# Moving a share of dense work into a fifth stage of a graph network, with a third-layer term computed early

## The reference

```python
h = jnp.maximum(_layernorm(x, axis=-1), 0.0)
x = x + _L0_gnn_ref(h, src, dst, W_neigh1, W_self1, b_self1, ...)   # three layers of:
    neigh_sum = segment_sum(h[src], dst); h_neigh = neigh_sum * inv_deg
    h @ W_self.T + b_self + h_neigh @ W_neigh.T          # relu after the first two
h = jnp.maximum(_layernorm(x, axis=-1), 0.0)
x = x + _L1_gnn_ref(h, edge_attr_128, src, dst, W_O, b_O, W_I, b_I, W_S, b_S, gamma, beta)
    ho = mean over dst of (h[src] - edge_attr); hi = mean over src of (h[dst] - edge_attr)
    hh = (ho @ W_O.T + b_O + hi @ W_I.T + b_I + h @ W_S.T + b_S) / 3, then normalised over the nodes
```

## Time and profile before

| | us |
|---|---|
| median of three runs | 5942.0 |
| the three runs | 5934.94, 5942.0, 5949.29 |
| the profiled execution | 5937.81 |
| its span, first to last instruction | 5936.1 |
| PE, DVE, ACT, POOL busy | 4546.6, 4002.2, 2957.0, 3686.2 |

### The profile page before, as it was taken

How to read it: one execution, slowest core, us unless ns; L and a number is a source line. 1 busy time by engine, 2 the same in 40 slices (tenths; PEclk the granted TensorE clock), 3 DMA queues, 4 the chain that set the end, 5 groups by cost and what they waited for, 6 DMA issues and landing times. The chain is left out here.

```text
span 5936.1 us, 109947 instructions
## 1 busy us (share of the span) xinstructions
PE 4546.6 (77%) x24681; PEld 3377.0 (57%) x24851; DVE 4002.2 (67%) x15228; ACT 2957.0 (50%) x6894; POOL 3686.2 (62%) x3909
## 2 busy tenths in 40 slices
PE   3894956668998998735767745989999997777675
PEld 1573644446686687634655523876666664333675
DVE  4884855555785687844358737759999997666552
ACT  0494755553684585533211100548888884444432
POOL 0466667760570372075777831758888877887587
PEclk9997977779999999955999978559999997889897
DMA  3363546668887887854677678544444444443564
GB/s 104 125 212 108 184 150 210 207 197 266 279 290 251 283 292 257 294 148 151 234 222 156 129 168 220 157 139 171 171 171 171 171 143 150 123 126 107 128 120 65
DMA packets 701876, 1075.70 MB, mean 181 GB/s; under 512 B 101651, under 2 KB 384517, under 8 KB 701340
## 3 DMA queue, kind: packets, MB, share of 16 engines
q1 hardware_dynamic: 528090, 833.70, 42.6%
q0 software_dynamic: 137600, 175.02, 14.3%
q10 hardware_dynamic: 36000, 64.94, 2.9%
HBM read 652.09 MB, written 443.26 MB: 185 GB/s over the span
## 5 line engine op out<-in xcount | busy, mean ns | idle before, releaser
L1097 POOL DMA_INDIRECT G_x<-node_table,G_idx x400 | 396.3, 991 | 569.1 <-ACT G_idx L1083 448.0
L1097 POOL DMA_INDIRECT G_V<-layer_rows,G_idx x400 | 381.5, 954 | 124.1 <-issue 111.8
L1126 PE MATMUL bank<-first_last_indicators,G_V 125*128 (+1 forms) x1600 | 273.3, 293 | 179.5 <-DVE G_V L1774 179.4
L1126 PEld LDWEIGHTS bank<-first_last_indicators,G_V 125*128 125x128 f32 x1600 | 277.5, 261 | 183.6 <-issue 130.9
L1954 POOL DMA_INDIRECT node_table<-H_out,H_idx x200 | 324.3, 1622 | 91.8 <-issue 56.9
L1954 POOL DMA_INDIRECT out<-O_out,O_idx x200 | 316.7, 1583 | 104.0 <-issue 59.9
L1474 PE MATMUL bank<-B_S,B_V 127*128 127x125 f32 x2000 | 290.9, 291 | 80.0 <-DVE B_S L1450 37.4
L2726 ACT ACTIVATE P_h<-P_x,P_nb,P_rs 128x128 f32<-128x128 f32 x784 | 320.2, 479 | 0.0
L1474 PEld LDWEIGHTS bank<-B_S,B_V 127*128 127x128 f32 x2000 | 261.0, 203 | 100.7 <-issue 74.9
L2645 POOL TENSOR_TENSOR P_gA<-P_x,bn_scale 128x512 f32<-128x512 f32 x196 | 250.7, 1279 | 65.8 <-DMA P_x<-node_table 42.2
L1078 POOL COPY G_idx<-i_tb 128x4 int32 (+1 forms) x100 | 20.8, 209 | 428.1 <-POOLq L257 427.6
(11 more groups left out here) (486 smaller groups left out, 14848.4 us busy)
## 6 DMA issues: line engine op xcount, KB each, us to landing
P_x<-node_table SPq DMA_DIRECT2D x196, 512.0 KB
B_V<-values SPq DMA_DIRECT2D x250, 256.0 KB, 4.5
BN_g<-node_table SPq DMA_DIRECT2D x195, 256.0 KB
out<-P_out SPq DMA_DIRECT2D x195, 256.0 KB
node_table<-G_xg SPq DMA_DIRECT2D x97, 512.0 KB
values<-G_V SPq DMA_DIRECT2D x150, 256.0 KB
layer_rows<-A_a SPq DMA_DIRECT2D x100, 256.0 KB, 3.2
layer_rows<-B_rows SPq DMA_DIRECT2D x100, 256.0 KB
```

What stands on the lines that cost most here:

```text
L1097: pool.indirect_dma_start(out=rows[u][:, c, :], out_offset=None, in_=table, in_offset=bass.IndirectOffsetOnAxis(ap=idx[u][:, c:c + 1], axi ...
L1126: last = nc.tensor.matmul(m.bank[7][:, bass.ds((i * TILE + c) * 2, 2)], V[0:EP, c, :], m.ind[0:EP, bass.ds(i * TILE + c, 1), :].rearrange( ...
```

## The change

1. `SHARES = (43, 43, 43, 43, 24)` takes the place of four quarters: positions, lookup, G1 and G2 have 43 dense groups beside them for 49, and G3 has the last 24.
2. `together` no longer writes all bodies up to the last end of any part: when the shortest part has ended, it starts again with those that are left, and gives them a loop if there is room. `beside` takes a part for ACT and the number of bodies in a turn, eight in G3.
3. "A" computes more: for every edge's source, x + b3 + (second layer) self3, as if it had no neighbours. PE has one bias matmul and four self3 matmuls a step behind its other work, DVE an addition with x, SP a store of 256 KB. They go to the second half of a new table TB3 of the third layer, the first half of which B3 fills as it filled X1. `x_src` has eight slots, and the gather of step i waits also for the x1 of step i-8.
4. "G3" gathers from TB3 with `i_tb`, so it needs no dense row, and `i_src2` with its three operations is dropped. Its work is spread over more bodies: the root in body i+1, the scale in i+2, the normalisation in i+3, the subtraction in i+4, the sums and the store in i+5. `x` has eight slots, and the gather waits for step i-8. The index column of step i+3 is copied by ACT behind the root of step i-1.

The core of the diff:

```diff
-CHUNKS = 4
+SHARES = (43, 43, 43, 43, 24)
...
-            nc.vector.scalar_tensor_tensor(t1[:], csrc[:], -2.0, tb[:], ALU.mult, ALU.add).then_inc(s_f, 1)
-            dve.wait_ge(s_f, 5)
-            nc.vector.scalar_tensor_tensor(hi_f[:], t1[:], 2.0 * N, t2[:], ALU.add, ALU.mult).then_inc(s_f, 1)
-            dve.wait_ge(s_f, 6)
-            nc.vector.scalar_tensor_tensor(m.i_src2[0:EP], csrc[:], 2.0, hi_f[:], ALU.mult, ALU.add).then_inc(s_f, 1)
...
@@ edges_start, gpsimd @@
-                    f.landed(s_xo, i - 4, u)
-                    gather(pool, f, idx_s, s_is, i, u, a["x"], xs_whole, s_gs)
+                    f.landed(s_xo, i - 4, u % 4)
+                    f.after(s_x1, i - 8)
+                    w = u % 4
+                    gather(pool, f, idx_s, s_is, i, w, a["x"], xs_whole[u - w:u - w + 4], s_gs)
@@ edges_start, vector @@
+                        f.after(s_m3, i - 5)
+                        f.landed(s_3o, i - 9, v)
+                        nc.vector.tensor_tensor(x1[v][:], r3[0:EP, :].rearrange("p (c f) -> p c f", c=TILE), xs[(w - 5) % 8][:], ALU.add)\
+                          .then_inc(s_x1, 1)
@@ edges_start, tensor @@
+                        f.after(s_x1, i - 6)
+                        nc.tensor.matmul(r3[0:EP, :], m.ones16[:, 0:EP], m.b3parts[:], start=True, stop=False, skip_group_check=True)
+                        for c in range(TILE):
+                            last = nc.tensor.matmul(r3[0:EP, c * D:(c + 1) * D], a2T[(u - 5) % 4][:, c * EP:(c + 1) * EP], m.w["self3"],
+                                                    start=False, stop=True, skip_group_check=True)
+                        last.then_inc(s_m3, 1)
@@ incoming @@
+        def gpsimd(pool):
+            def body(i, u, has):
+                if has(i):
+                    f, w = Flow(pool, has, m), u % 4
+                    f.after(s_h, i - 8)
+                    gather(pool, f, idx, s_i, i, w, m.TB3, x_whole[u - w:u - w + 4], s_g)
...
+        def scalar(act):
+            def body(i, u, has):
+                f = Flow(act, has)
+                if has(i - 1):
+                    w = (u - 1) % 4
+                    ln.root(f, i - 1, w)
                     if has(i + 3):
+                        scalar_index(nc, m.i_tb, idx, s_i, i + 3, w)
+                if has(i - 3):
+                    v = (u - 3) % 4
+                    f.after(ln.s_nb, i - 3)
+                    f.after(s_v, i - 7)
+                    ln.relu(h[v], [x[(u - 3) % 8][:, c, :] for c in range(TILE)], v).then_inc(s_h, 1)
...
+        beside(nc, m, a, P, 4, sync=sync, vector=vector, scalar=scalar, gpsimd=gpsimd, tensor=tensor,
+               sync_once=lambda sp: sp.wait_ge(m.s_ea, m.ea_copied), sync_end=lambda sp: finish(sp, s_vo, n), unroll=8)
```

More of the change, by code:

```diff
@@ L50, in together, with step @@
 def together(eng, parts, unroll=4, back=3, ahead=3):
[L52 to L68 removed]
+    begin = min(p[0] for p in parts)
+    while parts:
+        start = unroll * -(-max(begin, back + 1) // unroll)
+        rounds = max(0, min((n - special - ahead - start) // unroll for _, n, _, special, _ in parts))
+        short = min(last for _, _, last, _, _ in parts)
+        end = start + unroll * rounds
+        stop = max(end, short + 1)
+        def step(i):
+            for first, n, last, _, body in parts:
+                if first <= i <= last:
+                    body(i, i % unroll, lambda g: 0 <= g < n)
+        for i in range(begin, start):
+            step(i)
+        if end > start:
+            with eng.Fori(start // unroll, end // unroll) as k:
+                for u in range(unroll):
+                    for _, _, _, _, body in parts:
+                        body(k * unroll + u, u, lambda g: True)
+        for i in range(end, stop):
+            step(i)
+        begin, parts = stop, [p for p in parts if p[2] >= stop]
 def slot_value(g, s, slots=4):
@@ L533, in __init__, with beside, in_fours @@
         self.sync, self.vector, self.scalar, self.tensor, self.stored = sync, vector, scalar, tensor, stored
-def beside(nc, m, a, P, chunk, sync=None, vector=None, gpsimd=None, tensor=None, sync_once=None, sync_end=None, vector_end=None,
-           gpsimd_end=None):
+def beside(nc, m, a, P, chunk, sync=None, vector=None, scalar=None, gpsimd=None, tensor=None, sync_once=None, sync_end=None, vector_end=None,
+           gpsimd_end=None, unroll=4):
     groups = -(-m.N // ROWS)
-    first = chunk * groups // CHUNKS
-    dense = DenseFirst(nc, m, a, P, first, (chunk + 1) * groups // CHUNKS - first)
+    borders = [sum(SHARES[:k]) * groups // sum(SHARES) for k in range(len(SHARES) + 1)]
+    first = borders[chunk]
+    dense = DenseFirst(nc, m, a, P, first, borders[chunk + 1] - first)
+    def in_fours(part):
+        first, n, last, special, body = part
+        return first, n, last, special, lambda i, u, has: body(i, u % 4, has)
     def sweeps(eng, own, other, first_other=False):
-        together(eng, ([other(eng)] if other and first_other else []) + ([own(eng)] if own else []) + ([other(eng)] if other and not first_other else []),
-                 back=7, ahead=4)
+        together(eng, ([other(eng)] if other and first_other else []) + ([in_fours(own(eng))] if own else [])
+                 + ([other(eng)] if other and not first_other else []), unroll=unroll, back=7, ahead=4)
     with nc.Block() as block:
@@ L1378, in _ @@
                 pads_clear(P, act)
-                sweep(act, 0, n, n + 3, body, back=8, ahead=4, special=0)
+                sweep(act, 0, n, n + 3, body, unroll=8, back=8, ahead=4, special=0)
             @block.tensor
@@ new lines, in vector, with body @@
+        def vector(dve):
+            def body(i, u, has):
+                f = Flow(dve, has)
+                if has(i - 2):
+                    ln.finish(f, i - 2, (u - 2) % 4)
+                if has(i):
+                    f.landed(s_g, i, u % 4, 64)
+                    ln.stats(dve, f, i, u % 4, [x[u][:, c, :] for c in range(TILE)])
+                if has(i - 4):
+                    v = (u - 4) % 4
+                    f.after(s_h, i - 4)
+                    f.landed(s_e, i - 4, v)
+                    f.landed(s_vo, i - 8, v)
+                    f.after(s_hl, i - 8)
+                    nc.vector.tensor_tensor(V[v][:], h[v][:], ea[v][:], ALU.subtract).then_inc(s_v, 1)
+            clear_pads(nc, P, dve)
+            return 0, n, n + 3, 0, body
```

143 lines of the change are left out of this document (48 added, 95 removed).

## The result

| | us |
|---|---|
| before, median of 16 runs | 5943.95 |
| after, median of 16 runs | 5929.36 |
| ratio, 95% interval | 0.9978 (0.9971 to 0.9986) |
| profiled executions, before and after | 5937.81 and 5925.57 |

The account below looks back on a forecast made before the run. No engine is busy throughout; each stage, behind barriers, is bound by its own last engine. Terms -7 - 34 + 4.5 + 32 = -4.5 us on 5942.0 give 5937.5, say 5938; range 5920 to 5966.

Parts of the forecast that it names:

- Positions: Stage positions: POOL ends it alone, so fewer dense groups gain nothing, at most 1 us.
- Lookup, G1, G2: These three stages: dense groups end them; with fewer, lookup gains 7 us and G1 and G2 17 us each.
- A: Stage A: POOL sets the pace at 9.98 us a step, so the added steady work costs 0.
- The drain of +4.5: End of A: added matmuls and addition lie on the path behind the last gather, +4.5 us (bounds +2, +10).
- G3: Stage G3 with 24 dense groups: full bodies of 6.9 us, 294.6 us for 262.4, +32 us (bounds +27, +45).
- The sum: All touched stages together: -4.5 us.
- First: Rival in G3: DVE and ACT hold each other up, body 8.2 us, 23 us more, 5961; chance 0.17.
- Second: Rival in G3: PE loses its clock, +9 us (5947) or, at half clock, +56 (5994); chance 0.07.
- Third: Rival in A: PE binds at the half clock, +32 us, 5970; chance 0.07.
- Fourth: Rival in G1 and G2: GpSimd's steps quicken to 5.03 us, another 8 to 10 us each, 5920; chance 0.12.

Follow-up runs that it names:

- values_first: Changed kernel with VectorE's subtraction in G3 moved ahead of the wait for new rows and their statistics; 5924.15 us, ratio 0.997.
- before_58_at128: Kernel before with shares 58, 46, 46, 46 and an unused tile of 96 bytes a partition; 5906.4 us.
- before_58_shift: Kernel before with shares 58, 46, 46, 46 and an unused tile of 32 bytes a partition; 5908.05 us, ratio 0.994.
- after_shift: Changed kernel with an unused tile of 32 bytes a partition; 5938.37 us, ratio 0.999.
- act_plus: Changed kernel with one more ScalarE copy, 0.19 us, in each step of G3, to a tile nobody reads; ratio 0.9978.
- padded: Changed kernel with the node table allocated at its former size in DRAM; 6472.58 us, ratio 0.9778, on the third chip.
- g3_alone: Changed kernel with shares 49, 49, 49, 49, 0, so G3 runs without dense groups; 6544.68 us, ratio 0.9903, on the third chip.

## Why the prediction was right, and where it was not

**Positions** keeps its length with 43 groups, and even with 58: right, and worth more than the prediction made of it.

**Lookup, G1, G2** ended on the dense groups, and these are gone from the end: right. What is late next was named wrongly in all three. In lookup the forecast took DVE's table rows (-7), in the layer stages the landing of the last store (-17 each). Both steps overlooked GpSimd's release, 8.8 to 8.9 us behind the end of its last gather. (The store that the forecast took is indeed over before: SP is through at 1800.5, GpSimd at 1804.4.) From the earlier trace rows that is 800.40 + 0.94 + 8.83 = 810.2 for 812.70, -2.5, and -2.3 was measured; from the earlier trace rows 1795.81 + 8.89 = 1804.7 for 1818.60, -13.9, and -15.3 and -13.6 were measured. The term was 10 us too large over the three stages. In the kernel before, positions is the one touched stage that GpSimd's drain ends (last scatter to the next stage 10.2 us), and there the prediction didn't ask what follows POOL's last instruction.

**A**: the steady step costs nothing, as forecast (9.99 us in all kernels, and GpSimd waits for x1 20 times by 0.3 us in 480, without a longer step). The drain of +4.5 isn't established, though the two profiles differ by 4.3. Without the third chip, A takes 535.7, 535.9, 537.4, 538.9, 539.9 us in kernels with the old code and 536.2, 536.3, 539.7, 539.9, 540.0 with the new: means 0.9 us apart in a scatter of 4. What scatters is the drain: from A's first gather to the end of its last it is 499.0 to 499.6 us in all ten. In the changed kernel and in values_first, whose A is the same, the clock goes with it. The same stretch of both:

```profile
1319.00:1328.00 9.00, 8.35 (x28) 6.39 (x29) 1.19 (x2) 4.95 (x12) 0.00 (x0) 0.50 0.21 81
```

```profile
1320.00:1328.00 8.00, 8.00 (x54) 6.34 (x53) 2.56 (x4) 4.35 (x10) 0.00 (x0) 1.00 0.60 229
```

At the lower level (1.2 GHz) PE did 28 matmuls in 9 us, at the upper (2.4 GHz) 54 in 8; from the last gather to the end it is 39.6 us in the one and 35.9 in the other. But the clock is not all of it. The whole drain of before_58_at128 and of before_58_shift, with equal code in A:

```profile
1310.40:1346.00 35.60, 24.87 (x110) 18.68 (x108) 14.74 (x44) 13.52 (x29) 0.02 (x1) 0.75 0.37 138
1312.80:1350.80 38.00, 20.94 (x110) 14.77 (x110) 14.37 (x44) 13.52 (x29) 0.02 (x1) 0.85 0.38 141
```

The one with the lower mean clock is the shorter. What sets the length of the drain stays open. That the two profiles differ by nearly my +4.5 is luck; five traces of either kind put the term at 1 us and don't tell it from nothing.

**G3**, counted from its first gather:

| | forecast | measured |
|---|---|---|
| first statistics | +9 | +8.5 |
| a full body | 6.9 | 6.46 |
| gather 25 goes out | +155 | +148.5 |
| gather 30 goes out | +183 | +175.9 |
| twenty gathers from there, each | 5.03 | 5.18 |
| end of the last gather to the next stage | 11 | 14.3 |
| sum | 294.6 | 293.8 |

The body fell below the lower bound of 6.63: I had added a dense body's and an edge body's busy time from different stages. The lengths of DVE's rows still add up as I had it (8.6 us a body, for 5.9 and 2.8), but in company more of them overlap, and the time that they cover is 6.2 us (124.2 in 20 bodies) for 6.63. POOL waits for ACT's index copy as forecast:

```profile
POOL G_x L1103 <- ACT G_idx L1089: 26.6, 17, 1.6
```

By gather 30 that had made the stage 7 us shorter than forecast. Two terms gave it back: the stretched gathers, +3, and the drain, +3.3, in which the last three bodies are normalised one behind the other:

```profile
2767.51 4.71 ACT L1227 ACTIVATE G_h<-G_x,G_ln_nb,G_ln_rs 125x128 f32<-125x128 f32 x12
...
2768.86 4.44 SPq L1772 DMA_DIRECT2D values<-G_V  x4
...
2777.68 0.84 DVE L1150 COPY G_shared_first_last<-bank 128x400 f32<-128x400 f32 x1 [4.74 <-PEq L264]
```

So G3's +31.3 is near the forecast's +32 by errors that cancel, which is luck. Without dense groups the new form still takes 8 us more than the old one; of the 31 us only 22 are the dense work.

**The sum** of the touched stages came to +3.5 for -4.5, by the releases. What the prediction priced thus made the kernel slower and not faster; that the whole went the way of the forecast is luck. That the profiled time is 7.7 us below the forecast all the same (-12.2 for -4.5; the medians differ by 2.4 us more) is the batch norm's 11.4 us, for which no step of the prediction stood, and 3.5 us in B3, G4 and P3. Those last were not tested. G4 takes 287.1 to 293.6 us from one kernel's trace to another's. P3 is not such a scatter: it is 1.4 to 3.2 us longer in after, after_shift, values_first, act_plus, padded and g3_alone than in the other eight, and why stays open. The prediction asked which rows the change touches, and a change of SBUF addresses touches all stages behind it.

**The rivals.** First: no, 6.46 us a body and not 8.2. Second: no, the clock is 1.00 through the full bodies. (Its price at the half clock was low: 5.4 us at half speed are 10.8, not 10.) Third: no, PE is at 68% and GpSimd's steps keep their length. Fourth: no, the steps of G1 are as long as before (5.27 us); only the last four come down to 5.0 to 5.1.

## What to carry to other kernels

Where GpSimd's indirect DMAs end a stage, count 8.9 us from the end of the last gather to the next stage (10.2 behind the scatters of positions) before moving other engines' work away from that end; what finishes inside that time is free. Ask first which stage has room: 24 dense groups cost 22 us beside G3, while 15 more beside positions cost 2.4 us at most, and 3 more in each of the next stages 1.6 us at most. The room depends on the chip too: on the third one 15 more beside positions cost over 70 us. When tiles are filled by transfers of 512-byte pieces, start them at a multiple of 256 bytes, and look at the addresses of every stage behind a tile that is added or dropped.

## What was not expected of the hardware

- The place of a tile in SBUF sets the rate of the transfers that fill it: 310 GB/s at a multiple of 256 bytes, 290 at 32, 64, 128 or 288 over one of 512, the same on three chips.
- An indirect DMA of GpSimd that starts under VectorE's TENSOR_TENSOR on two SBUF operands ends 0.82 us after that instruction, in 34 of 34 long ones (alone it takes 0.94 us); one that has begun isn't touched, nor one under a TENSOR_TENSOR with an operand in PSUM.
- GpSimd's drain ends 7.9 us after its last gather (9.3 after the scatters of positions), and 8.82 to 8.89 us lie between the end of that gather and the first instruction behind the barrier wherever nothing else is later.
- One chip takes 6613 us for a kernel that takes 5942 elsewhere, with gaps of 1.1 us between VectorE's instructions that nothing in the profile explains.
